# Feed-forward weights turned by transposing DMAs behind the output stores, with the first matrix in four column blocks, in place of TensorE transposes

## The chip, the core and the metric

One core of one Trainium2 chip. The metric is the device time of one execution in microseconds. A profiled execution has a span (first to last instruction) and a time of its own, which is a little longer. TensorE's clock has two levels, 1.2 and 2.4 GHz; the profile gives the granted clock of a stretch as a share of full speed.

## What is computed

A decoder layer with layer normalisation after each of three parts, for x of 16 x 256 x 512 in float32:

```python
x = _layernorm(x + attn(x, ...))               # gated long convolution (Hyena)
x = _layernorm(x + xattn(ctx, ctx, x, ...))     # state-space kernel, 32 heads of 8 rows
x = _layernorm(x + ffn(x, w1, w2))

def _bitlinear(x, w):                           # w1: 2048 x 512, w2: 512 x 2048
    rms = rsqrt(max(mean(w * w), EPS))
    w_quant = clip(round(w * rms), -1, 1) / rms
    scale = 127 / max(max(abs(x), -1), EPS)
    x_quant = clip(round(x * scale), -128, 127) / scale
    return einsum('bsd,fd->bsf', x_quant, w_quant)
# ffn: _bitlinear(gelu(_bitlinear(x, w1)), w2)
```

The weights are thus -1, 0 or 1 times a scalar. TensorE contracts over partitions, so both matrices must lie in SBUF transposed: w1 with its 512 input dims on partitions (4 groups of 128), w2 with its 2048 (16 groups).

## The kernel before

It runs as two blocks of five engine programs, one behind the other with a barrier of all engines between. `hyena_block` computes the first part, in two halves of 128 batch rows (HALF = 2), and leaves its result in HBM (`x1_scratch`). `heads_block` does the second and third part in a software pipeline over 32 heads. The change lies in the last stage of `hyena_block`, in the second half.

**A half.** 24 slots (two per group of 128 channels and kind x1, v, x0) project x with f16 matmuls (L509), ScalarE and VectorE form the short convolution, and for each of four channel groups a long convolution goes through HBM (`regroup`, `bring_back`). Then 16 output tokens follow. For each token R, TensorE multiplies y by `wout_t` into one of four half banks of `slot_bank` (`out_part`, L546; a float32 matmul is two records, so eight of a token); the first three of four partial products of tokens 0 to 3 are made ahead. `out_part(R)` waits until VectorE has added token R - 4. VectorE adds the residual row group `res` (L857), measures it (L859, L861), GpSimd makes the inverse deviation (L1050, L1052), and VectorE normalises one token later (L866). `res` has four buffers.

**SP's queue in this stage** (L446 to L454) is a hand-written order: for each t, `load_res(R + 3)`, which waits until the store of token R - 1 has landed, then `store_res(R)`, which waits for L866. All DMAs of the kernel are issued by SP and share one hardware queue. Ahead of the stage stand the loads of the weight parts 2 to 6 and of the first ctx, toeplitz and x1 data of the next block; part 7 is loaded at t = 0.

**The weights.** The two matrices go in eight parts of 128 x 2048 float32 (four of w1, four of w2). In the second half's slots ScalarE squares them for the mean; later each part is loaded again into `part_raw[i]` (buffers that are free by then), ScalarE rounds it (`round_part`, L749; the rounded number stands in the low half word of the float32), and VectorE clips it (`clip_part`, L954; parts 2 to 7 behind tokens 1 to 6). Then TensorE turns it: `turn_part(i)` (L589 to L601) does 16 transposes of 128x128 f16 into two PSUM banks behind token t = 1 + i (`PART_AT`), and ScalarE copies both halves out (`copy_part`, L751 to L760), subtracting the offset 1536, into `w1_t` or `w2_t`, which lie over `x_hi` and `x_lo`. ScalarE's order is round part i + 2, copy part i. Behind the last token `turn_first_ctx` and `convolve_first` do the first pieces of the next block in the same banks.

**The second block** turns its activations with transposing DMAs: `turn_xq` (L1328, 128x512 f16) and `turn_hq` (L1332, twice 128x1024 f16 a head), fed by ScalarE's `pack_xq` and `pack_hq` (L1538, L1515), which are passes of the same form as the new `pack_part`. `ffn1` (L1442) reads `w1_t` in rows of 512, `ffn2` (L1421) reads `w2_t`.

Of the kernel before, what the change touches and what calls it, by code (L numbers as in the profile page):

```python
# [6 lines left out]
ACT = mybir.ActivationFunctionType  # L7
AX_X = mybir.AxisListType.X
F32 = mybir.dt.float32
F16 = mybir.dt.float16  # L10
# [3 lines left out]
P = 128  # L14
T, B, D = 16, 256, 512
DC = D // P
E = 3 * D
EC = E // P
F = 2048
FC = F // P  # L20
# [4 lines left out]
HALF = B // P  # L25
# [13 lines left out]
HALF_ONE = 1536.0  # L39
# [3 lines left out]
def view(ap, offset, *dims):  # L43

    return bass.AP(ap.tensor, ap.offset + offset, [ap.ap[0], *[list(d) for d in dims]])
# [3 lines left out]
def hyena_block(nc, w, early, dram):  # L49
# [8 lines left out]
    NSLOT = 2 * 3 * DC  # L58
# [14 lines left out]
    PARTS = 4  # L73
    with ExitStack() as ctx:
# [6 lines left out]
        def sem(name):  # L81
            return ctx.enter_context(nc.semaphore(name))
# [6 lines left out]
        x_hi, x_lo = w["x_hi"], w["x_lo"]  # L89
# [3 lines left out]
        v_tok = sb("v_tok", [P, P * T])  # L93
# [33 lines left out]
                    *[view(w[name][:, :, :].bitcast(F32), 0, (1, F)) for name in ("w_hi", "w_lo")],  # L127
                    view(u[:, :, :], 0, (1, F)), view(conv_all[:, :, :, :], X0 * F, (1, F))]

        turn_bank = [view(early["conv_bank"][i // 2][:, i % 2, :], 0, (P, 4), (1, P)) for i in range(4)]  # L130
        slot_bank = [ps(f"slot_bank{i}", [P, 2, 512]) for i in range(2)]

# [13 lines left out]
        slot_full = sem("slot_full")  # L146
# [7 lines left out]
        c_stored = sem("c_stored")  # L154
        c_loaded = sem("c_loaded")
        ch_full = sem("ch_full")
        ch_copied = sem("ch_copied")
# [44 lines left out]
        inv_made = sem("inv_made")  # L202
        clipped = sem("clipped")
        rounded = sem("rounded")
        part_turned = sem("part_turned")
        part_done = sem("part_done")

        def quad_buf(Q):
# [6 lines left out]
        TOTAL_AT, SUM_MATRIX_AT, MEAN_AT, INVERSE_AT = 18, 19, 20, 21  # L215
        ROUND_AT = {21: 0, 23: 1}
        CLIP_AT = {i - 1: i for i in range(2, 2 * PARTS)}
        PART_AT = {1 + i: i for i in range(2 * PARTS)}
        CTX_AT, PAIRS_AT = 11, 12

        TURN_AT = {4: 1, 9: 2, 14: 3}
# [47 lines left out]
        with nc.Block() as block:  # L269
            @block.sync  # L270
            def _(sp):
# [66 lines left out]
                def load_part(i):  # L338
# [12 lines left out]
                        sp.wait_ge(y_done, 4 * HALF * DC)  # L351
                    sp.dma_start(part_target(i, part_raw[i]), part_source(i)).then_inc(part_loaded[i], 16)

                def load_w_in(cc):
                    for k in range(KINDS):
                        e = k * DC + cc
                        sp.dma_start(raw_w_in(KINDS * cc + k), dram["W_in"][e * P:(e + 1) * P, :]).then_inc(win_loaded[cc], 16)
# [53 lines left out]
                for hf in range(HALF):  # L411
# [34 lines left out]
                    for t in range(T):  # L446
                        R = hf * T + t
                        if R + 3 < HALF * T:
                            load_res(R + 3)
                        store_res(R)  # L450
                        if hf + 1 < HALF and t in LOAD_QUAD_AT:
                            load_quad(NQ * (hf + 1) + LOAD_QUAD_AT[t])
                        if hf + 1 == HALF and t == 0:
                            load_part(2 * PARTS - 1)  # L454

            @block.tensor
            def _(pe):
# [128 lines left out]
                    pe.wait_ge(ch_copied, 4 * (HALF * DC - 1))  # L586
                    nc.tensor.matmul(turn_bank[0][:, 0, 0:2], ones[:, :], total[:, :], start=True, stop=True).then_inc(summed, 1)

                def turn_part(i):  # L589
                    pe.wait_ge(clipped, i + 1)  # L590
                    low = view(part_raw[i].bitcast(F16), 0, (2, F))
                    for hh in range(2):
                        if i >= 2:
                            pe.wait_ge(part_done, 2 * (i - 2) + hh + 1)
                        elif hh == 0:
                            pe.wait_ge(ch_copied, 4 * HALF * DC)
                        out = turn_bank[2 * (i % 2) + hh][:, :, :].rearrange("p a b -> p (a b)").bitcast(F16)
                        for j in range(FC // 2):
                            fc = hh * FC // 2 + j
                            last = nc.tensor.transpose(out[:, j * P:(j + 1) * P], low[:, fc * P:(fc + 1) * P], w["ident16"][:, :])  # L600
                        last.then_inc(part_turned, 1)  # L601

                def turn_first_ctx():
                    pe.wait_ge(early["ctx_reversed"], 1)
                    pe.wait_ge(part_done, 2 * (2 * PARTS - 2) + 1)
                    for lb in range(LB):
                        last = nc.tensor.transpose(turn_bank[0][:, lb, :], early["ctx_rev"][:, 0, lb * P:(lb + 1) * P], w["ident"][:, :])
                    last.then_inc(early["ctx_turned"], 1)

                def convolve_first(tb):  # L610

                    if tb == 0:
                        pe.wait_ge(early["toep_loaded"][0], 16)
                        pe.wait_ge(early["kv_done"], 1)
                        pe.wait_ge(part_done, 2 * 2 * PARTS)
                    for sb_ in range(tb + 1):
                        for hh in range(2):
                            last = first_conv(nc, early, turn_bank[2 * tb + hh][:, :, :].rearrange("p a b -> p (a b)"), tb, sb_, hh)
                    last.then_inc(early["conv_full"], 1)
# [7 lines left out]
                for hf in range(HALF):  # L627
# [25 lines left out]
                        out_part(hf * T + t, range(DC - 1))  # L653
                    for t in range(T):
                        out_part(hf * T + t, range(DC) if t >= PARTIAL else [DC - 1])
                        if hf + 1 == HALF and t in PART_AT:
                            turn_part(PART_AT[t])
                        if hf + 1 == HALF and t == CTX_AT:
                            turn_first_ctx()
                        if hf + 1 < HALF and t in QUAD_AT:  # L660
                            turn_quad(NQ * (hf + 1) + QUAD_AT[t])
# [5 lines left out]
            def _(act):  # L667
# [80 lines left out]
                    m = i // PARTS  # L748
                    nc.scalar.activation(part_raw[i], part_raw[i], ACT.Copy, scale=rms[:, m:m + 1], bias=LOW_HALF).then_inc(rounded, 1)  # L749

                def copy_part(i):  # L751
                    for hh in range(2):
                        act.wait_ge(part_turned, 2 * i + hh + 1)
                        bank = turn_bank[2 * (i % 2) + hh][:, :, :].rearrange("p a b -> p (a b)").bitcast(F16)
                        if i < PARTS:
                            out = view(w["w1_t"], (4 * i + 2 * hh) * P, (P, 2), (F, DC), (1, P))
                        else:
                            out = view(w["w2_t"], hh * (FC // 2) * D + (i - PARTS) * P, (D, FC // 2), (1, P))
                        src = view(bank, 0, (DC * P, 2), (P, DC), (1, P)) if i < PARTS else view(bank, 0, (P, FC // 2), (1, P))
                        nc.scalar.activation(out, src, ACT.Copy, bias=-HALF_ONE).then_inc(part_done, 1)  # L760

                norm_first(0)
                split_hi(0)
# [28 lines left out]
                for i in range(2 * PARTS):  # L792
                    if i + 2 < 2 * PARTS:
                        round_part(i + 2)
                    copy_part(i)
                for h in range(2):
                    act.wait_ge(early["ctx_loaded"][h], 16)
                    reverse_blocks(nc, early, h).then_inc(early["ctx_reversed"], 1)
# [367 lines left out]
def heads_block(nc, w, early, dram):  # L1166
# [6 lines left out]
    with ExitStack() as ctx:  # L1173
# [115 lines left out]
        with nc.Block() as block:  # L1289
# [72 lines left out]
            def _(pe):  # L1362
# [61 lines left out]
                def ffn1(head, k):  # L1424
# [14 lines left out]
                    else:  # L1439
                        pe.wait_ge(g_done, head.count(4, 2))  # L1440
                    for dc in range(DC):
                        last = nc.tensor.matmul(bank[:, :], xq_t[:, dc, :], w["w1_t"][:, dc, k * 512:(k + 1) * 512],  # L1442
                                                start=(dc == 0), stop=(dc == DC - 1))
                    last.then_inc(ff1_full, 1)

# [352 lines left out]
def build(nc, dram):  # L1798
    with ExitStack() as ctx:
# [6 lines left out]
            "block_diag": sb("block_diag", [P, GROUPS, P]),  # L1806
            "x_hi": sb("x_hi", [P, DC, T * P], F16), "x_lo": sb("x_lo", [P, DC, T * P], F16),
        }
        w["w1_t"] = w["x_hi"][:, :, :]
        w["w2_t"] = w["x_lo"][:, :, :].rearrange("p c (k e) -> p (c k) e", e=D)  # L1810

        early = {name: view(w["block_diag"][:, :, :], n * 2 * L, *dims) for n, (name, dims) in enumerate((
# [59 lines left out]
```

## Time and profile before

| | us |
|---|---|
| median of 3 runs | 1064.82 (1059.51 to 1065.6) |
| the profiled execution | 1063.69 |
| its span | 1061.9 |
| TensorE matmul / weight load, busy | 1006.2 / 602.9 |
| VectorE / ScalarE / GpSimd, busy | 799.3 / 599.9 / 552.7 |

In the rows below, times are in us from the span's start and mean durations in ns unless marked. PE is TensorE's matmuls, PEld its weight loads, DVE VectorE, ACT ScalarE, POOL GpSimd, SPq SyncE's queue of DMA issues. A row of the timeline has start, duration, engine, line, operation, output<-input, count, and in square brackets the idle time before it with what ended it. The profile names, for a wait on several semaphores, the one that came last. A row of the windows has the stretch, its length, each engine's busy time with the count of instructions, then the granted clock, the mean busy share of the 16 DMA engines, and GB/s.

### The profile page before, as it was taken

What the parts mean: (1) busy time and instruction counts of PE and PEld (TensorE: products, weight loads), DVE (VectorE), ACT (ScalarE), POOL (GpSimd) and SP (SyncE); (2) the same over time, 40 slices, a digit from 0 to 9 for tenths busy, and PEclk for the clock granted to TensorE, in tenths of its full rate; (3) what the DMA queues carried; (4) which work ended last, traced back from release to release, by engine and by line L of the source; (5) the groups of instructions that cost most, each with busy time, mean ns of one, the idle gap of its engine ahead of it and who ended that gap; (6) DMA issues with size and microseconds to landing.
All of it is one profiled execution on the core that took longest, in us unless ns stands there. A gap on an engine that the chain in (4) does not pass through costs nothing.

```text
span 1061.9 us, 14827 instructions
## 1 busy us (share of the span) xinstructions
PE 1006.2 (95%) x4679; PEld 602.9 (57%) x4679; DVE 799.3 (75%) x1509; ACT 599.9 (56%) x728; POOL 552.7 (52%) x886
## 2 busy tenths in 40 slices
PE   3899999999999999978999999999999999999985
PEld 2455545544445555456666666666666666666641
DVE  7967975786475567657888888888888888888862
ACT  5655544112566558114666666767576767676664
POOL 5320310221000004269787887878787878787861
PEclk9999999999999999989999999999999999999998
DMA  9323655456475777441444544444444444444334
GB/s 322 61 60 120 203 152 163 145 165 194 162 227 189 241 259 255 141 143 51 105 98 113 105 113 108 115 106 117 104 117 105 109 114 101 122 99 114 76 64 91
DMA packets 178220, 144.65 MB, mean 136 GB/s; under 512 B 99988, under 2 KB 132792, under 8 KB 176120
## 3 DMA queue, kind: packets, MB, share of 16 engines
q1 hardware_dynamic: 178168, 144.00, 49.3%
q8 instruction: 27, 0.44, 0.2%
q14 instruction: 25, 0.20, 0.1%
HBM read 89.29 MB, written 33.70 MB: 116 GB/s over the span
## 4 chain that ended last, share of the span: by engine, by line
PE 50%; DVE 2%; POOL 1%; ACT 1%; DMA 1%; issue 1%; POOLq 0%; DVEq 0%; ACTq 0%
PE conv_bank L1398 28%; PE hq_bank L1421 9%; PE ff_bank L1442 5%; PE back_bank L1442 5%; PE back_bank L1412 1%; PE back_bank L1381 1%; PE ctx_bank L1369 1%; DMA hq_t<-hq_int 0%; POOL sum L1742 0%; DVE z L1607 0%; DVE g_max L1674 0%; POOL sum L1744 0%; ACT g L1546 0%; DMA xq_t<-xq_int 0%; ACT hq_f L1507 0%
## 5 line engine op out<-in xcount | busy, mean ns | idle before, releaser
L1742 POOL TENSOR_TENSOR sum<-z 128x640 f32<-128x640 f32 x128 | 198.2, 1549 | 11.6 <-DVE z L1619 9.6
L837 DVE SCALAR_TENSOR_TENSOR conv_all<-u,taps,conv_all 128x1024 f32<-128x1024 f32 x92 | 122.4, 1331 | 93.2 <-ACT conv_all L708 91.4
L1398 PE MATMUL conv_bank<-block_diag 128*128 128x288 f32 x628 | 167.8, 411 | 1.8 <-DVE z L1619 1.8
L1398 PE MATMUL conv_bank<-kv,block_diag 128*128 128x288 f32 x640 | 168.6, 406 | 0.9 <-DVE z L1619 0.8
L1398 PEld LDWEIGHTS conv_bank<-kv,block_diag 128*128 128x128 f32 x640 | 117.8, 190 | 31.6 <-DVE z L1619 1.8
L1398 PEld LDWEIGHTS conv_bank<-block_diag 128*128 128x128 f32 x628 | 117.3, 193 | 32.4 <-DVE z L1619 2.2
L1421 PE MATMUL hq_bank<-x_lo,hq_t 128*128 128x512 f16 x512 | 122.2, 382 | 4.7 <-DMA hq_t<-hq_int 4.7
L1674 DVE TENSOR_REDUCE g_max<-g 128x1 f32<-128x512 f32 x128 | 85.8, 673 | 41.5 <-ACT g L1546 41.5
L700 ACT ACTIVATE u<-slot_bank,bias,unscale 128x1024 f32<-128x1024 f32 x46 | 55.4, 1204 | 108.9 <-PE slot_bank L509 88.6
L1744 POOL TENSOR_TENSOR sum<-sum 128x320 f32<-128x320 f32 x128 | 111.3, 869 | 10.0
L1607 DVE TENSOR_TENSOR z<-conv_bank,qx 128x512 f32<-128x512 f32 x128 | 88.0, 687 | 34.2 <-PE conv_bank L1398 24.6
L546 PE MATMUL slot_bank<-wout_t,y 128*128 128x512 f32 x256 | 112.8, 594 | 0.0
L1520 ACT ACTIVATE x<-x,a_shift,a_rstd 128x512 f32<-128x512 f32 x32 | 26.0, 814 | 134.9 <-POOL a_shift L1763 134.9
L509 PE MATMUL slot_bank<-x_hi,w_hi 128*128 128x512 f16 x384 | 91.8, 381 | 3.8 <-ACT conv_all L708 2.1
L509 PE MATMUL slot_bank<-x_lo,w_hi 128*128 128x512 f16 x384 | 91.2, 379 | 3.5 <-DVE x_lo L825 3.5
L509 PE MATMUL slot_bank<-x_hi,w_lo 128*128 128x512 f16 x384 | 91.9, 382 | 0.0
L1050 POOL TENSOR_SCALAR r_rstd<-r_meanvar 128x1 f32<-128x1 f32 x32 | 19.7, 614 | 134.2 <-DVE r_meanvar L861 134.2
L1421 PEld LDWEIGHTS hq_bank<-x_lo,hq_t 128*128 128x128 f16 x512 | 50.1, 98 | 64.8 <-DMA hq_t<-hq_int 6.5
L546 PEld LDWEIGHTS slot_bank<-wout_t,y 128*128 128x128 f32 x256 | 47.6, 190 | 54.3 <-issue 54.0
L1507 ACT ACTIVATE hq_f<-g,h_scale 128x1024 f32<-128x1024 f32 x64 | 73.0, 1141 | 2.0 <-DVE h_scale L1669 2.0
L1442 PE MATMUL ff_bank<-x_hi,xq_t 128*128 128x512 f16 x256 | 66.6, 383 | 3.4 <-DMA xq_t<-xq_int 3.4
L1616 DVE TENSOR_TENSOR z<-conv_bank,qx 128x384 f32<-128x384 f32 x128 | 69.3, 542 | 0.0
(181 smaller groups left out, 1676.2 us busy)
## 6 DMA issues: line engine op xcount, KB each, us to landing
x_quad<-in_w SPq DMA_DIRECT2D x10, 1024.0 KB, 8.3
v_scratch<-conv_all SPq DMA_DIRECT2D x16, 512.0 KB, 3.5
c_scratch<-v_tok SPq DMA_DIRECT2D x8, 1024.0 KB, 5.3
y<-c_scratch SPq DMA_DIRECT2D x8, 1024.0 KB, 4.9
res<-in_x SPq DMA_DIRECT2D x32, 256.0 KB, 2.9
x_scratch<-res SPq DMA_DIRECT2D x32, 256.0 KB, 3.1
block_diag<-in_ctx SPq DMA_DIRECT2D x32, 256.0 KB, 3.7
block_diag<-ssm_scratch SPq DMA_DIRECT2D x32, 256.0 KB, 3.7
```

The lines of the kernel that those rows point to most:

```text
L509: last = nc.tensor.matmul(slot_bank[n % 2][:, q, :], wt[:, dc, e * P:(e + 1) * P], xt[:, dc, cols], start=(j == 0 and dc == 0), stop=(j == ...
L546: last = nc.tensor.matmul(slot_bank[R // 2 % 2][:, R % 2, :], y[:, cc, t, :], w["wout_t"][:, cc, :], start=(cc == 0), stop=(cc == DC - 1))
L837: ins = nc.vector.scalar_tensor_tensor(out=acc, in0=(u_first[kind] if n < 3 else u)[:, t0 + tap:t0 + tap + T // 2, :].rearrange("p t b -> ...
L1398: last = nc.tensor.matmul(view(conv_bank[tb % 2][:, hh, :], 0, (ROW64, T // 2), (1, PAIRS)), toep[:, head.buf, (tb - sb_) * P:(tb - sb_ + ...
L1421: last = nc.tensor.matmul(hq_bank[:, :], hq_t[:, fc, :], w["w2_t"][:, fc, :], start=(fc == 0), stop=(fc == FC - 1))
L1442: last = nc.tensor.matmul(bank[:, :], xq_t[:, dc, :], w["w1_t"][:, dc, k * 512:(k + 1) * 512], start=(dc == 0), stop=(dc == DC - 1))
L1507: nc.scalar.activation(hq_f[:, half], g[:, half], ACT.Copy, scale=h_scale[:, 0:1], bias=LOW_HALF).then_inc(hq_rounded, 1)
L1607: nc.vector.tensor_tensor(view(z[:, b, :, :], 0, (4 * PLANE, T), (PLANE + 1, 4), (1, HD)), view(conv, 0, (ROW64, T), (HD, 4), (1, HD)), vi ...
L1616: nc.vector.tensor_tensor(view(z[:, b, :, :], DN, (4 * PLANE, T), (PLANE, 3), (1, HD)), view(conv, HD, (ROW64, T), (HD, 3), (1, HD)), view ...
L1674: nc.vector.tensor_reduce(g_max[:, k:k + 1], g[:, k * 512:(k + 1) * 512], AX_X, ALU.max, apply_absolute_value=True).then_inc(g_maxed, 1)
L1742: nc.gpsimd.tensor_tensor(sum2[:, :, :], z[:, b, :, 0:half], z[:, b, :, half:2 * half], ALU.add).then_inc(sum2_done, 1)
L1744: nc.gpsimd.tensor_tensor(sum1[:, :, :], sum2[:, :, 0:PLANE], sum2[:, :, PLANE:half], ALU.add).then_inc(sum1_done, 1)
```

## The change

Each part, once clipped, is packed by ScalarE (`pack_part`) into f16 in SBUF, into a buffer that is free by then (`part_int`: v_tok, and then the first half of the raw buffer of the part before). SP then issues one transposing DMA per part (`turn_part`, now in SP's program) from there into `w1_t` or `w2_t`, at the end of the iterations t = 2 to 9. `w1_t` is laid out as [k, dc, 512] in place of [dc, k x 512], and for w1 the pack puts the four 128-column blocks of a row group in the order in which the DMA can write them in one run. TensorE's 128 transposes and ScalarE's 16 copies from PSUM are removed, with the waits of `turn_first_ctx` and `convolve_first` on them. SP waits at the end of its program for all eight.

```diff
@@ -126,6 +126,8 @@
                     *[view(conv_all[:, :, :, :], n * F, (1, F)) for n in (X1, V)],
                     *[view(w[name][:, :, :].bitcast(F32), 0, (1, F)) for name in ("w_hi", "w_lo")],
                     view(u[:, :, :], 0, (1, F)), view(conv_all[:, :, :, :], X0 * F, (1, F))]
+
+        part_int = [view(home, 0, (1, F // 2)).bitcast(F16) for home in (v_tok[:, :], *part_raw[:-1])]
 
         turn_bank = [view(early["conv_bank"][i // 2][:, i % 2, :], 0, (P, 4), (1, P)) for i in range(4)]
         slot_bank = [ps(f"slot_bank{i}", [P, 2, 512]) for i in range(2)]
@@ -202,7 +204,7 @@
         inv_made = sem("inv_made")
         clipped = sem("clipped")
         rounded = sem("rounded")
-        part_turned = sem("part_turned")
+        packed = sem("packed")
         part_done = sem("part_done")
 
         def quad_buf(Q):
@@ -215,7 +217,7 @@
         TOTAL_AT, SUM_MATRIX_AT, MEAN_AT, INVERSE_AT = 18, 19, 20, 21
         ROUND_AT = {21: 0, 23: 1}
         CLIP_AT = {i - 1: i for i in range(2, 2 * PARTS)}
-        PART_AT = {1 + i: i for i in range(2 * PARTS)}
+        TURN_PART_AT = {2 + i: i for i in range(2 * PARTS)}
         CTX_AT, PAIRS_AT = 11, 12
 
         TURN_AT = {4: 1, 9: 2, 14: 3}
@@ -350,6 +352,17 @@
                     elif i == 7:
                         sp.wait_ge(y_done, 4 * HALF * DC)
                     sp.dma_start(part_target(i, part_raw[i]), part_source(i)).then_inc(part_loaded[i], 16)
+
+                def turn_part(i):
+
+                    if i == 0:
+                        sp.wait_ge(slot_full, HALF * NSLOT)
+                    sp.wait_ge(packed, i + 1)
+                    if i < PARTS:
+                        out = view(w["w1_t"], i * DC * 512, (P, FC), (1, P))
+                    else:
+                        out = view(w["w2_t"], (i - PARTS) * P, (D, FC), (1, P))
+                    sp.dma_start_transpose(out, part_int[i]).then_inc(part_done, 16)
 
                 def load_w_in(cc):
                     for k in range(KINDS):
@@ -452,6 +465,9 @@
                             load_quad(NQ * (hf + 1) + LOAD_QUAD_AT[t])
                         if hf + 1 == HALF and t == 0:
                             load_part(2 * PARTS - 1)
+                        if hf + 1 == HALF and t in TURN_PART_AT:
+                            turn_part(TURN_PART_AT[t])
+                sp.wait_ge(part_done, 2 * PARTS * 16)
 
             @block.tensor
             def _(pe):
@@ -586,23 +602,9 @@
                     pe.wait_ge(ch_copied, 4 * (HALF * DC - 1))
                     nc.tensor.matmul(turn_bank[0][:, 0, 0:2], ones[:, :], total[:, :], start=True, stop=True).then_inc(summed, 1)
 
-                def turn_part(i):
-                    pe.wait_ge(clipped, i + 1)
-                    low = view(part_raw[i].bitcast(F16), 0, (2, F))
-                    for hh in range(2):
-                        if i >= 2:
-                            pe.wait_ge(part_done, 2 * (i - 2) + hh + 1)
-                        elif hh == 0:
-                            pe.wait_ge(ch_copied, 4 * HALF * DC)
-                        out = turn_bank[2 * (i % 2) + hh][:, :, :].rearrange("p a b -> p (a b)").bitcast(F16)
-                        for j in range(FC // 2):
-                            fc = hh * FC // 2 + j
-                            last = nc.tensor.transpose(out[:, j * P:(j + 1) * P], low[:, fc * P:(fc + 1) * P], w["ident16"][:, :])
-                        last.then_inc(part_turned, 1)
-
                 def turn_first_ctx():
                     pe.wait_ge(early["ctx_reversed"], 1)
-                    pe.wait_ge(part_done, 2 * (2 * PARTS - 2) + 1)
+                    pe.wait_ge(ch_copied, 4 * HALF * DC)
                     for lb in range(LB):
                         last = nc.tensor.transpose(turn_bank[0][:, lb, :], early["ctx_rev"][:, 0, lb * P:(lb + 1) * P], w["ident"][:, :])
                     last.then_inc(early["ctx_turned"], 1)
@@ -612,7 +614,6 @@
                     if tb == 0:
                         pe.wait_ge(early["toep_loaded"][0], 16)
                         pe.wait_ge(early["kv_done"], 1)
-                        pe.wait_ge(part_done, 2 * 2 * PARTS)
                     for sb_ in range(tb + 1):
                         for hh in range(2):
                             last = first_conv(nc, early, turn_bank[2 * tb + hh][:, :, :].rearrange("p a b -> p (a b)"), tb, sb_, hh)
@@ -653,8 +654,6 @@
                         out_part(hf * T + t, range(DC - 1))
                     for t in range(T):
                         out_part(hf * T + t, range(DC) if t >= PARTIAL else [DC - 1])
-                        if hf + 1 == HALF and t in PART_AT:
-                            turn_part(PART_AT[t])
                         if hf + 1 == HALF and t == CTX_AT:
                             turn_first_ctx()
                         if hf + 1 < HALF and t in QUAD_AT:
@@ -748,16 +747,19 @@
                     m = i // PARTS
                     nc.scalar.activation(part_raw[i], part_raw[i], ACT.Copy, scale=rms[:, m:m + 1], bias=LOW_HALF).then_inc(rounded, 1)
 
-                def copy_part(i):
-                    for hh in range(2):
-                        act.wait_ge(part_turned, 2 * i + hh + 1)
-                        bank = turn_bank[2 * (i % 2) + hh][:, :, :].rearrange("p a b -> p (a b)").bitcast(F16)
-                        if i < PARTS:
-                            out = view(w["w1_t"], (4 * i + 2 * hh) * P, (P, 2), (F, DC), (1, P))
-                        else:
-                            out = view(w["w2_t"], hh * (FC // 2) * D + (i - PARTS) * P, (D, FC // 2), (1, P))
-                        src = view(bank, 0, (DC * P, 2), (P, DC), (1, P)) if i < PARTS else view(bank, 0, (P, FC // 2), (1, P))
-                        nc.scalar.activation(out, src, ACT.Copy, bias=-HALF_ONE).then_inc(part_done, 1)
+                def pack_part(i):
+
+                    act.wait_ge(clipped, i + 1)
+                    if i == 0:
+                        act.wait_ge(c_stored, 16 * HALF * DC)
+                    else:
+                        act.wait_ge(packed, i)
+                    low = view(part_raw[i].bitcast(F16), 0, (2, F))
+                    if i < PARTS:
+                        out, src = view(part_int[i], 0, (DC * P, DC), (P, DC), (1, P)), view(low, 0, (2 * P, DC), (2 * D, DC), (2, P))
+                    else:
+                        out, src = part_int[i], low
+                    nc.scalar.activation(out, src, ACT.Copy, bias=-HALF_ONE).then_inc(packed, 1)
 
                 norm_first(0)
                 split_hi(0)
@@ -792,7 +794,7 @@
                 for i in range(2 * PARTS):
                     if i + 2 < 2 * PARTS:
                         round_part(i + 2)
-                    copy_part(i)
+                    pack_part(i)
                 for h in range(2):
                     act.wait_ge(early["ctx_loaded"][h], 16)
                     reverse_blocks(nc, early, h).then_inc(early["ctx_reversed"], 1)
@@ -1439,7 +1441,7 @@
                     else:
                         pe.wait_ge(g_done, head.count(4, 2))
                     for dc in range(DC):
-                        last = nc.tensor.matmul(bank[:, :], xq_t[:, dc, :], w["w1_t"][:, dc, k * 512:(k + 1) * 512],
+                        last = nc.tensor.matmul(bank[:, :], xq_t[:, dc, :], w["w1_t"][:, k, dc, :],
                                                 start=(dc == 0), stop=(dc == DC - 1))
                     last.then_inc(ff1_full, 1)
 
@@ -1806,7 +1808,7 @@
             "block_diag": sb("block_diag", [P, GROUPS, P]),
             "x_hi": sb("x_hi", [P, DC, T * P], F16), "x_lo": sb("x_lo", [P, DC, T * P], F16),
         }
-        w["w1_t"] = w["x_hi"][:, :, :]
+        w["w1_t"] = view(w["x_hi"][:, :, :], 0, (DC * 512, F // 512), (512, DC), (1, 512))
         w["w2_t"] = w["x_lo"][:, :, :].rearrange("p c (k e) -> p (c k) e", e=D)
 
         early = {name: view(w["block_diag"][:, :, :], n * 2 * L, *dims) for n, (name, dims) in enumerate((
```

## Rows read from the trace of the kernel before

**Rows 1.** The page: busy time by engine, and the chain that ended last.
```profile
PE 1006.2 (95%) x4679; PEld 602.9 (57%) x4679; DVE 799.3 (75%) x1509; ACT 599.9 (56%) x728; POOL 552.7 (52%) x886
...
PE 50%; DVE 2%; POOL 1%; ACT 1%; DMA 1%; issue 1%; POOLq 0%; DVEq 0%; ACTq 0%
```

**Rows 2.** Waits from 411 to 462 us, then VectorE's timeline.
```profile
DVE res L857 <- DMA res<-in_x: 15.5, 13, 2.9
...
429.26 0.69 DVE L857 TENSOR_TENSOR res<-slot_bank,res 128x512 f32<-128x512 f32 x1 [1.35 <-DMA res<-in_x]
...
455.76 0.69 DVE L857 TENSOR_TENSOR res<-slot_bank,res 128x512 f32<-128x512 f32 x1 [1.35 <-DMA res<-in_x]
```

**Rows 3.** Timeline of SP's queue of DMA issues.
```profile
411.84 0.33 SPq L283 DMA_DIRECT2D res<-in_x  x1
...
429.87 0.33 SPq L283 DMA_DIRECT2D res<-in_x  x1
430.24 0.43 SPq L288 DMA_DIRECT2D x_scratch<-res  x1
433.37 0.33 SPq L283 DMA_DIRECT2D res<-in_x  x1
...
440.75 0.43 SPq L288 DMA_DIRECT2D x_scratch<-res  x1
445.79 0.33 SPq L283 DMA_DIRECT2D res<-in_x  x1
```

**Rows 4.** Line L288, the stores: time from issue to landing.
```profile
DMA to landing us min/median/max: 2.0/3.1/7.6
```

**Rows 5.** Timeline of TensorE: token 8, the turn of part 7, token 9.
```profile
424.21 3.65 PE L546 MATMUL slot_bank<-wout_t,y 128*128 128x512 f32 x8
427.70 1.06 PE L600 MATMUL conv_bank<-ident,conv_all 128*128 128x128 f16 x16
428.59 3.65 PE L546 MATMUL slot_bank<-wout_t,y 128*128 128x512 f32 x8
```

**Rows 6.** Timeline of ScalarE, then lines L1515 and L1538 (min/median/max ns).
```profile
393.47 1.99 ACT L749 ACTIVATE conv_all<-conv_all,rms 128x2048 f32<-128x2048 f32 x1
...
423.96 1.94 ACT L760 ACTIVATE x_lo<-conv_bank 128x1024 f16<-128x1024 f16 x2 [1.60 <-PE conv_bank L600]
...
L1515 ACT ACTIVATE hq_int<-hq_f x64: 1045/1057/1060, 505.4 to 1047.0; 128x1024 f16<-128x1024 f16 x64
...
L1538 ACT ACTIVATE xq_int<-xq_f x32: 629/630/631, 486.0 to 1033.0; 128x512 f16<-128x512 f16 x32
```

**Rows 7.** The transposing DMAs of 1024 and 512 columns, and one's stretch.
```profile
L1332 SPq DMA_TRANSPOSE hq_t<-hq_int x64: 1232/1252/2031, 506.5 to 1048.1; - x64
...
DMA to landing us min/median/max: 3.0/3.1/4.8
...
L1328 SPq DMA_TRANSPOSE xq_t<-xq_int x32: 1190/1213/1324, 486.6 to 1033.7; - x32
...
DMA to landing us min/median/max: 2.4/2.4/2.5
...
503.20:504.40 1.20, 1.20 (x8) 1.00 (x8) 1.10 (x6) 0.19 (x1) 1.06 (x2) 1.00 0.48 107
```

**Rows 8.** Windows: eight tokens of the output stage.
```profile
412.00:440.00 28.00, 27.73 (x124) 14.15 (x123) 20.01 (x36) 15.68 (x16) 12.27 (x16) 1.00 0.53 159
```

**Rows 9.** Timeline of SP's queue in the first half, around a 1 MB load.
```profile
204.54 0.43 SPq L276 DMA_DIRECT2D x_quad<-in_x  x1
207.58 0.33 SPq L283 DMA_DIRECT2D res<-in_x  x1
...
213.90 0.33 SPq L283 DMA_DIRECT2D res<-in_x  x1
```

**Rows 10.** Windows: TensorE's granted clock around the start of the second block.
```profile
456.20:459.90 3.70, 0.00 (x0) 0.00 (x0) 2.11 (x5) 0.00 (x0) 1.00 (x3) 0.86 0.26 97
...
466.00:468.00 2.00, 2.00 (x5) 1.43 (x5) 0.00 (x0) 0.00 (x0) 1.84 (x4) 0.50 0.72 215
```

## The prediction

> **What bounds the kernel now.** I read the page first: TensorE is busy for 1006.2 us of 1061.9, and the chain of waits gives it half of the span [rows 1]. That makes "less work on TensorE" look like time won. But the share is an average, and the change acts in one stage only, the last 16 output tokens of the first block (from 399 to 459 us), where the eight parts of the weights are turned. So I read that stage by its waits, then in order of time.
>
> In this stage VectorE's addition of the residual (L857), one per token, waits in 13 of 16 tokens, and each time for the same thing: the DMA that brings the residual row group into `res`. From token 8 (429.26) to token 15 (455.76) it never finds the row there early [rows 2]. TensorE is ahead of it: its last output matmul of token 8 ends near 427.7, 1.5 us before VectorE takes it up, and that with all eight turns in its stream.
>
> What sets the pace of these loads is SP's own order, `load_res(R + 3)`, `store_res(R)`: a load needs the buffer that the store of token R - 1 empties. The load at 429.87 is followed by the store at 430.24, and the next load goes out at 433.37, which is 3.1 us behind that store, the median time to landing of such a store [rows 3, 4]. So a token costs 0.37 + 3.1 = 3.5 us, whatever TensorE does. TensorE spends 427.70 - 424.21 = 3.5 us on a token and its wait for the bank, and 0.89 on a turn [rows 5]. Two places in the row depart from 3.5: up to 411.84 the DMA engines work off the weights and early context loads (I give this stretch no change: none of its transfers is touched), and the store at 440.75 takes 5.0 us, so that the next load comes at 445.79 [rows 3]. That straggler is worth 5.4 - 3.5 = 1.9 us here.
>
> **The change part by part.**
>
> *TensorE loses the turns.* A turn of one part takes 0.89 us of its stream (427.70 to 428.59) [rows 5]; eight make 7.1 us. Because from token 3 on VectorE takes tokens at the pace of the loads, and the four banks let TensorE run at most four tokens ahead, TensorE stands idle for those 7.1 us instead. Value at the end of the block: 0; were TensorE the pacer it would be -7.1.
>
> *ScalarE packs in place of copying.* Two copies of about 1 us from PSUM go (the pair at 423.96 takes 1.94), one pass of 128x2048 comes. The nearest rows are `pack_hq`, 1.06 us for 1024 columns, and `pack_xq`, 0.63 for 512, so 0.43 per 512 more and 1.06 + 2 x 0.43 = 1.9 us for 2048 [rows 6]. Even. ScalarE's waits for TensorE in this stage (1.60 before that pair) go too; it waits for the clips instead, which stay where they are in VectorE's order. Part 7 is clipped before VectorE takes up token 8 at 429.26 [rows 2], so the last pack is done by 431.2 at the latest. Nothing waits for ScalarE there. Value 0.
>
> *SP gets eight transposing DMAs*, one at the end of each of the iterations t = 2 to 9, behind `store_res(t)`. Their waits first: they would be reached from about 416.5 (t = 2) to 441 (t = 9), and the packs are done from 397 (part 0, behind the rounding that ends at 395.5 [rows 6], + 1.9) to 431 (part 7), some 10 us earlier or more. So SP doesn't stop at `packed`. If it did, the loads and stores of all later tokens would stand behind it, microsecond for microsecond. Issuing: 1.21 us for 512 columns, 1.25 for 1024 [rows 7]; for 2048 I take 1.3 (by the same step; the other end is 4 x 1.21 = 4.9, if the issue went by size). It falls into the 3.1 us in which SP waits for the store anyway. Value 0 by the first; by the second the turn's issue ends 0.43 (the store's own issue) + 4.9 = 5.3 us behind the store, 2.2 more than 3.1, and eight add +18. I hold that far off, since doubling the size adds 0.04.
>
> *The data that they move* is the term that counts. A turn of 512 columns (128 KB) keeps the 16 DMA engines 0.48 x 1.20 = 0.58 us at full share and moves 107 GB/s x 1.2 us, which is all of it [rows 7]. A part has 2048 columns, so 4 x 0.58 = 2.3 us; by the landing times (3.1 for 1024 columns, 2.4 for 512) each 512 more take 0.7, so 2.8. I take 2.45. The loads and stores of eight tokens take 0.53 x 28 us, 1.85 a token [rows 8]. Together 4.3 us of work a token, more than the 3.5 in which a token goes by now. In order of time: the store goes out at 0, the turn's data runs behind it from about 2 to 4.5, the next load and store (issued at 3.1 and 3.5) come behind it and land near 7.4, in place of 6.6. So a token costs 4.3 for as long as a turn stands in each, and the eight add 8 x 0.8 = +6.4 us. Low end: 0, if the turn's data slips into the pauses of the engines (they are idle for half of the time [rows 8]). High end by the nearest row of a big transfer at the same place: the 1 MB load of `x_quad` issued at 204.54 behind a store in the first half; the period after it is 213.90 - 207.58 = 6.3, which is 2.8 more than 3.5 [rows 9]. Half its size at its rate: 1.4 each, +11; at its full price +22.
>
> The Trainium skill would have this term vanish. "Advanced Engine Details and Errata", section "X-Bar Transpose (TRN2)", says that such DMAs are about as fast as plain ones and expects 350 to 400 GB/s; a part would then take about 1.4 us as an estimate by that page, 3.3 with the token's own traffic, less than 3.5, and the time would stay. The trace speaks against it: over the whole stretch with any traffic of the 128 KB turn the engines are counted at 0.58 us, some 225 GB/s [rows 7].
>
> *TensorE's clock.* In the 3.7 us in which TensorE stands idle before the second block the granted clock is 0.86 on average, and it is at 0.50 (the 1.2 GHz level) still in 466 to 468 [rows 10]. After the change TensorE finishes the first block earlier against VectorE, so it idles longer before the same start; the start is at the low level already. Value 0; were the low level to last 4 us longer, up to 2 us more.
>
> *The new order of the first matrix* (column blocks) leaves each matmul's 512 columns contiguous; the second block reads, waits and issues as before. Value 0. The last transfer of a turn is issued about six tokens before the block's end, so the new last wait of SP is over when it is reached.
>
> **Sum.** 1063.69 (the profiled execution: span 1061.9 and 1.8 around it) + 6.4 = 1070.1 us. The median of the three runs is 1064.82, so this is 0.5% slower. A measurement of this kernel tells about 1% from no change.
>
> **The rivals.**
>
> A. *The turns pace the loads* (the forecast): a turn of 2.3 to 2.8 us of data adds 0.65 to 1.15 a token, so 1069 to 1073, or from 1067 on if the straggler is absent; 1070.1 at the price taken.
>
> B. *Hidden in the pauses.* The engines' share is only 0.53 here [rows 8], and the store is issued ahead of the turn. If the turn's data is through before the next store's turn comes, the token stays at 3.5: 1063.7, or 1061.8 if the straggler at 440.75 is absent. It takes a turn of under 3.5 - 1.85 = 1.65 us, against 2.3 by the row. By the page of the Trainium skill named above this would be the outcome.
>
> C. *The turns cost as the big load did*, 1.4 or more each, since reads and writes of three transfers in a queue mix badly: 1063.7 + 11 = 1075, at the full 2.8 each 1086. The second matrix's turns write 16 separate pieces of 128 elements into each partition, which no row shows.
>
> D. *TensorE is the pacer after all* and its 7.1 us come off: 1056.6; this is the side of faster. For it: tokens 4 to 8 took TensorE 4.4 us each with the turn. Against it: VectorE's waits name the load in all of them [rows 2]. It decides only if the loads land before the matmuls; they would have to be 0.9 us quicker per token.
>
> E. *The change doesn't get its cover*: a turn is not ready or its issue grows with the size, and SP stands still in front of loads and stores: +18, 1082.
>
> **How the numbers follow.** A 0.52, B 0.24, C 0.13, D 0.06, E 0.05. Slower by over 1% is above 1075.5: E with 0.05, two thirds of C (whose first price lies just under it) with 0.09, a little of A with 0.01, so 0.15. Faster by over 1% is below 1054.2, more than D gives: 0.03. Within 1%: 0.82. The range takes in B and, above, C's first price: 1060 to 1078.
>
> **What would show it.** Right: SP's issue rows hold eight transposing DMAs at 1.3 us each from t = 2; the loads at their side follow each other at 4.2 to 4.4 us and return to 3.5 from t = 10; DMA share above 0.9 in this stretch; VectorE still waits for `res<-in_x`; TensorE shows pauses for `slot_bank`; ScalarE's pack takes 1.9; the second block starts near 466 in place of 459.9 and lasts as long as before. Wrong: a cadence of 3.5 beside the turns (B) or 4.9 and more (C), stores landing later than 3.1 in iterations without a turn, or a second block that changes in length, which no step here foresees.

## The result, and the profile after

| | before | changed |
|---|---|---|
| median of six runs, us | 1065.38 (1059.51 to 1066.35) | 1072.11 (1070.84 to 1073.59) |
| ratio | | 1.0071, 95% interval 1.0047 to 1.0094 |
| profiled execution / its span | 1063.69 / 1061.9 | 1073.59 / 1071.8 |

The changed kernel is 0.7% slower. TensorE's counted busy time falls by 1.4 us, not by the 7.1 us of its turns, and the span is 9.9 us longer. The 1.4 says little by itself: over the profiles below that have the same 4551 matmul records, the busy time varies from 998.3 to 1005.1 us. First the page of the changed kernel (busy time, DMA queue), for [rows 1]:

```profile
PE 1004.8 (94%) x4551; PEld 598.6 (56%) x4551; DVE 799.9 (75%) x1509; ACT 600.5 (56%) x720; POOL 552.9 (52%) x886
...
q1 hardware_dynamic: 194808, 148.19, 51.0%
```

The 4.19 MB more than before in the queue (144.00 MB there) are the eight turns, 512 KB each. The timeline of SP's queue shows what they do to the loads, for [rows 3]:

```profile
413.86 0.33 SPq L285 DMA_DIRECT2D res<-in_x  x1
...
417.84 0.33 SPq L285 DMA_DIRECT2D res<-in_x  x1
418.21 0.43 SPq L290 DMA_DIRECT2D x_scratch<-res  x1
418.75 3.60 SPq L365 DMA_TRANSPOSE x_hi<-v_tok  x1
422.41 0.56 SPq L285 DMA_DIRECT2D res<-in_x  x1
...
452.48 2.95 SPq L365 DMA_TRANSPOSE x_lo<-u  x1
455.48 0.94 SPq L285 DMA_DIRECT2D res<-in_x  x1
...
459.81 0.33 SPq L285 DMA_DIRECT2D res<-in_x  x1
460.18 0.43 SPq L290 DMA_DIRECT2D x_scratch<-res  x1
463.26 0.33 SPq L285 DMA_DIRECT2D res<-in_x  x1
```

From 417.84 to 455.48 there are eight periods, each with a turn: 4.7 us each in place of 3.5. Behind the last turn one period of 4.3 follows, then 3.45 (459.81 to 463.26). What was not foreseen is the turn's own issue, 2.8 to 4.0 us instead of 1.3: in six of the eight periods store, turn and load stand in SP's queue without a pause, and the load goes out as soon as the issue of the turn has ended. The windows of that stretch, and the waits from 411 to 470 us, for [rows 8] and [rows 2]:

```profile
417.84:455.48 37.64, 30.19 (x70) 12.16 (x68) 19.60 (x37) 10.28 (x8) 11.22 (x16) 1.00 0.95 214
```
```profile
DVE res L859 <- DMA res<-in_x: 24.2, 12, 3.3
...
PE slot_bank L562 <- DVE res L859: 6.4, 6, 1.3
```

The DMA engines went from a share of 0.53 to 0.95. VectorE still waits for the residual loads, and longer. TensorE, 7.1 us of work lighter, now waits 6.4 us for VectorE to free a bank. ScalarE's pack takes 1.9 us, as worked out, and waits for nothing that matters (ScalarE's timeline, for [rows 6]):

```profile
429.18 1.91 ACT L762 ACTIVATE u<-conv_all 128x2048 f16<-128x2048 f16 x1 [3.21 <-DVE conv_all L956]
```

Where the 9.9 us of span came from: 2.0 stood already at the first undisturbed load (413.86 against 411.84), before any turn; 8.5 came in the stage (from that load to the second block's first transposes, 56.6 us against 48.1); and the second block is 0.6 shorter (601.4 against 602.0). The 2.0 are spread between executions: in the profiles of the ten experiments the same load lies anywhere from 408.67 to 414.79. So the stage is the better measure of one profile, and the medians (6.7 apart) are the fair total; the changed kernel's profile is the slowest of its six runs. The eight periods alone make 8 x 1.2 = 9.6. The straggler of 1.9 us in [rows 3] is absent here, and absent in e1 and e4 too, where SP's order of loads and stores is the same.

### The profile page after: what moved, and what is told of

Read it like the earlier page. It is cut to its first block, busy times and chain, and to the rows that moved or that the text cites. A ratio compares the mean times of both kernels' runs of the same rounds, so it can differ in the third digit from the quotient of the medians.

```text
span 1071.8 us, 14573 instructions
## 1 busy us (share of the span) xinstructions
PE 1004.8 (94%) x4551; PEld 598.6 (56%) x4551; DVE 799.9 (75%) x1509; ACT 600.5 (56%) x720; POOL 552.9 (52%) x886
## 4 chain that ended last, share of the span: by engine, by line
PE 50%; DVE 2%; POOL 1%; ACT 1%; DMA 1%; issue 0%; POOLq 0%; DVEq 0%; ACTq 0%
PE conv_bank L1400 27%; PE hq_bank L1423 10%; PE ff_bank L1444 5%; PE back_bank L1444 5%; PE back_bank L1414 1%; PE back_bank L1383 1%; PE ctx_bank L1371 1%; POOL sum L1744 0%; DVE z L1609 0%; DMA hq_t<-hq_int 0%; DVE g_max L1676 0%; POOL sum L1746 0%; ACT g L1548 0%; DMA xq_t<-xq_int 0%; POOL z L1778 0%
```

## The experiments

"Cadence" is the mean distance of the residual loads over eight periods beside the turns (where there are none, over the same tokens). "The block starts" is the second block's first transpose on TensorE: at 459.93 in the profile before, at 470.42 in the changed kernel's. All diffs are against the changed kernel unless said.

**e1_no_turns.** The eight transposing DMAs and their last wait are left out, so the feed-forward weights are never put in place; all the rest runs as in the changed kernel.

```diff
-                        if hf + 1 == HALF and t in TURN_PART_AT:
-                            turn_part(TURN_PART_AT[t])
-                sp.wait_ge(part_done, 2 * PARTS * 16)
```

> The eight transposing DMAs and the wait for them are left out (so the feed-forward weights are never put in place); TensorE's transposes are gone as in the changed kernel and ScalarE still packs. If the turns pace the loads (engines' work or SP's issue), the loads of res go out every 3.5 us through the whole stage again, and the time is that of the kernel before within its noise, 1062 to 1066: taking 7.1 us of work from TensorE is worth nothing. The rival, that TensorE's transposes were the pacer and the turns hide that gain, expects 1057 or less.

Measured: 1062.97 us, ratio to before 1.0005 (0.9986 to 1.0025). Its queue (timeline of SP):

```profile
429.12 0.33 SPq L285 DMA_DIRECT2D res<-in_x  x1
429.49 0.43 SPq L290 DMA_DIRECT2D x_scratch<-res  x1
432.56 0.33 SPq L285 DMA_DIRECT2D res<-in_x  x1
```

The cadence is 3.5 again. So the loss lies in the DMAs, and taking the transposes from TensorE is worth nothing in this kernel (within the interval). Rival D is out.

**e2_two_halves.** The same data at the same places, each turn cut into two DMAs.

```diff
-                    sp.dma_start_transpose(out, part_int[i]).then_inc(part_done, 16)
+                    for h in range(2):
+                        half = slice(h * FC // 2, (h + 1) * FC // 2)
+                        sp.dma_start_transpose(out[:, half, :], part_int[i][:, h * F // 2:(h + 1) * F // 2]).then_inc(part_done, 16)
```

> Each turn is issued as two DMAs of 1024 columns at the same place, the same data in all. Theory of the engines' work: the data sets the pace, so the cadence of the loads stays at 4.5 to 4.8 us beside the turns and the time at 1070 to 1074, however the issue is cut. Rival, issue by size: a DMA of 2048 columns costs SP 3.6 us because of its form, one of 1024 costs 1.25; two make 2.5, which fits into the 3.1 us of the store, and the cadence falls to 3.5 to 3.8, the time to 1064 to 1067.

Measured: 1069.57 us, 1.0052 (1.0035 to 1.0069). Timeline of SP and the windows of the stretch:

```profile
416.33 0.33 SPq L285 DMA_DIRECT2D res<-in_x  x1
416.70 0.43 SPq L290 DMA_DIRECT2D x_scratch<-res  x1
417.24 2.99 SPq L367 DMA_TRANSPOSE x_hi<-v_tok  x2
420.27 1.07 SPq L285 DMA_DIRECT2D res<-in_x  x1
...
450.93 0.78 SPq L285 DMA_DIRECT2D res<-in_x  x1
```
```profile
416.33:450.93 34.60, 30.34 (x70) 12.17 (x69) 19.50 (x36) 10.46 (x8) 11.21 (x16) 1.00 1.02 232
```

The cadence is 34.6 / 8 = 4.3 us, which is the sum of the prediction (2.45 + 1.85), with the engines' share at 1.02. That is a little under what was expected of the engines' work (4.5 to 4.8, 1070 to 1074). Issue by size would have given 3.5 to 3.8 and is out. In the two profiles one DMA of 2048 columns costs 0.4 a token more than two of 1024 with the same data, but the times don't confirm it: 1.0052 and 1.0071 have intervals that overlap.

**e3_act_issues.** SP's queue keeps loads and stores only; ScalarE issues the turns.

```diff
+                    if i >= 4:
+                        act.wait_ge(res_added, T + i + 1)
+                        turn_part(i - 4)
...
+                for i in range(4, 2 * PARTS):
+                    act.wait_ge(res_added, T + i + 5)
+                    turn_part(i)
```

> The same eight turns at about the same times, but issued from ScalarE's queue, so that SP's queue holds only loads and stores. Engines' work: SP is free, the engines still have about 4.5 us of work for a token, and the loads go out every 4.3 to 4.7 us; 1070 to 1074. Rival, SP's issue: SP no longer stands still, cadence 3.5, 1064 to 1066. If a second queue lets loads and stores pass the turns, the cadence lies near 3.5 as well, but then a turn lands later than 5.5 us.

Measured: 1076.34 us, 1.0122 (1.0105 to 1.0139). Timelines of SP and of ScalarE's queue:

```profile
425.22 0.33 SPq L285 DMA_DIRECT2D res<-in_x  x1
425.60 0.45 SPq L290 DMA_DIRECT2D x_scratch<-res  x1
430.34 0.33 SPq L285 DMA_DIRECT2D res<-in_x  x1
```
```profile
424.71 1.72 ACTq L760 DMA_TRANSPOSE x_hi<-x_quad  x1
```

SP is free, the turn's issue is short (1.4 to 2.2 us), and the cadence is 5.1, worse than in the changed kernel. A store issued at 425.60 lands only 4.7 us later. So the loss stays when SP is freed of the long issue. The expectation (4.3 to 4.7, 1070 to 1074) missed as well: that the second queue would be dearer by 0.4 a token than the first was in neither theory. Nor were the engines at their fullest: their share over the eight periods is 0.90, with 206 GB/s (windows):

```profile
414.98:455.83 40.85, 30.39 (x71) 12.43 (x69) 21.18 (x41) 10.57 (x8) 11.78 (x18) 1.00 0.90 206
```

**e4_turns_last.** The turns alone, behind the last store.

```diff
-                        if hf + 1 == HALF and t in TURN_PART_AT:
-                            turn_part(TURN_PART_AT[t])
+                for i in range(2 * PARTS):
+                    turn_part(i)
                 sp.wait_ge(part_done, 2 * PARTS * 16)
```

> All eight turns stand at the end of SP's program, behind the last store, with nothing beside them. Engines' work: the first is issued in about 1.3 us, since the queue is empty, and the later ones are held back to the pace of their data, some 2.5 us each; the second block starts 20 to 23 us after the last store, total near 1085. Issue by size: every one, the first too, is issued in 3 to 4 us, total near 1095. The loads of the stage go out every 3.5 us either way.

Measured: 1081.34 us in its one run (expected near 1085). Timeline of SP, and the windows of nearly all of it:

```profile
455.18 2.21 SPq L365 DMA_TRANSPOSE x_hi<-v_tok  x1
457.45 5.05 SPq L365 DMA_TRANSPOSE x_hi<-x_quad  x2
462.54 2.40 SPq L365 DMA_TRANSPOSE x_hi<-conv_all  x1
...
472.30 2.46 SPq L365 DMA_TRANSPOSE x_lo<-u  x1
```
```profile
455.18:474.70 19.52, 0.00 (x0) 0.00 (x0) 0.00 (x0) 0.00 (x0) 0.00 (x0) 0.50 1.09 209
```

Eight turns take from 455.18 to 474.76, 2.45 us each: the price taken in the prediction. Every turn lands 4.7 to 5.0 us after its issue began and the engines' share is 1.09, so they are held to the pace of their data. The first was expected at 1.3 us and took 2.2. But its queue was not empty: the last store had been issued at 454.76, 0.4 us before. In ScalarE's queue, which held nothing else in this stage (e3), the same turns were issued in as little as 1.35 us. So no run shows that the issue itself grows much from 1024 columns (1.25) to 2048. The loads of the stage kept 3.6. The second block starts at 477.61, some 23 us after the last store was issued, as expected (20 to 23).

**e5_spread.** Half turns as in e2, one a token, with four of them where no load follows. The schedule of the edit:

```diff
-        TURN_PART_AT = {2 + i: i for i in range(2 * PARTS)}
+        TURN_HALVES_AT = {**{t: (t - 1,) for t in range(1, 13)}, 13: (12, 13), 14: (14, 15)}
```

> The turns as sixteen DMAs of 1024 columns, one behind each store from t = 1 to 12 and two each at t = 13 and 14, where no load follows. Engines' work: half a turn is 1.2 us, with the token's own 1.85 it makes 3.1, less than the 3.5 of a token, so it is hidden: cadence of the loads 3.5 to 3.6, time 1062 to 1066, the changed kernel's loss gone with all its data still moved. Rival, that a transposing DMA in the queue costs each token a fixed delay whatever its size: 12 tokens at some 0.5 to 0.8 each, 1069 or more.

Measured: 1069.82 us, 1.004 (1.0022 to 1.0058). The expectation was wrong, and the time is the one that the rival gave (1069 or more), though not by its fixed delay of 0.5 to 0.8 a token. The cadence is (449.91 - 408.67) / 11 = 3.75, not 3.5, so 2.7 us; and the end of the stage is a new wait (timelines of SP, and of TensorE):

```profile
452.90 3.35 SPq L366 DMA_TRANSPOSE x_lo<-w_lo  x2
456.29 0.58 SPq L290 DMA_DIRECT2D x_scratch<-res  x1
456.92 2.74 SPq L366 DMA_TRANSPOSE x_lo<-u  x2
459.70 0.63 SPq L290 DMA_DIRECT2D x_scratch<-res  x1
```
```profile
462.27 1.09 PE L1385 MATMUL back_bank<-ident,block_diag 128*128 128x128 f32 x4 [9.87 <-PEq L271]
```

VectorE's last normalisation ended at 456.3, but the last stores stand in SP's queue behind four half turns: the block starts 6.0 us later instead of 0.8. "No load follows" was not enough; the stores and the barrier follow.

**e6_spread_swap, e7_before_swap, e8_after_swap, e9_no_turns_swap.** Four kernels with one more edit, the order of SP's queue in the second half: the store of token R goes out before the load of R + 3, so it no longer waits until the store before it has landed. e6 is e5 with it, e7 the kernel before, e8 the changed kernel, e9 is e1 (again without any turn, the weights not put in place).

```diff
                     for t in range(T):
                         R = hf * T + t
+                        if hf + 1 == HALF and t >= 1:
+                            store_res(R)
                         if R + 3 < HALF * T:
                             load_res(R + 3)
-                        store_res(R)
+                        if hf + 1 < HALF or t == 0:
+                            store_res(R)
```

> As e5_spread, and in the second half the store of token R stands ahead of the load of R + 3 in SP's queue, so that a store no longer waits for the landing of the one before. If SP's chain of store and load is the pacer of the stage, the cadence falls from 3.5 to 3.1 to 3.3 (then bound by the engines' 3.1 and the path normalise, store, load, add over three tokens) and the time to 1058 to 1062, since TensorE, without the transposes, can follow. Rival, that something else sets 3.5 (TensorE's 3.43 for a token, VectorE): no gain against e5_spread.

> The kernel before with the same exchange of store and load and nothing else. The loads' cadence falls as in e6_spread_swap, but now TensorE with its transposes ends token 15 only at 453 and becomes the pacer at the end: VectorE adds token 15 some 2 us earlier than before, 1061 to 1063. If it is as fast as e6_spread_swap, taking the transposes from TensorE is worth nothing even then; if not, the difference is what it is worth, at most 4 us.

> The changed kernel with the exchange. Engines' work: the engines are full beside the turns (share 0.95), so the order in the queue can give little: cadence 4.3 to 4.6 over the eight tokens, then shorter; time 1067 to 1071. Rival, SP's order and issue set 4.7: cadence falls to 4.0 or less, time 1065 or less.

> As e1_no_turns (the eight transposing DMAs and the wait for them left out, so the feed-forward weights are never put in place), with the store ahead of the load as in e7_before_swap. It shows what taking the transposes from TensorE is worth once the loads no longer pace the stage. In e7_before_swap VectorE waited 8.8 us for TensorE; without the transposes that goes, and the time should be 1 to 4 us under e7_before_swap (1056 to 1059). Rival: the loads and stores pace it at 3.1 us anyway and it is no faster than e7_before_swap, 1060.

Measured:

| | us | ratio to before, interval | cadence | block starts |
|---|---|---|---|---|
| e6_spread_swap | 1061.60 | 0.9979 (0.9963 to 0.9994) | 3.1 | 456.65 |
| e7_before_swap | 1059.99 | 0.9954 (0.9936 to 0.9972) | 3.3 | 454.91 |
| e8_after_swap | 1065.00 | 1.0003 (0.9988 to 1.0018) | 4.1 | 459.44 |
| e9_no_turns_swap | 1055.28 | 0.9922 (0.9900 to 0.9943) | 2.9 | 451.09 |

SP's chain was the pacer of the stage before: exchanging two lines of its queue gives 0.46%, somewhat more than expected (1059.99 against 1061 to 1063). In e7 VectorE's wait is now for TensorE (waits from 405 to 472 us of e7, for [rows 2]):

```profile
DVE res L860 <- PE slot_bank L549: 8.8, 7, 2.3
...
DVE res L860 <- DMA res<-in_x: 4.4, 3, 2.7
```

So once the loads are out of the way, TensorE's transposes do cost: e9 is 0.32% (3.4 us) faster than e7. The difference is only just clear of noise (0.04 to 0.60% by the two intervals, an estimate). And the turns cost more than that: e8, with them whole, is 0.8% above e9. In e8 the queue (timeline of SP, windows) is full at 4.1 a token:

```profile
421.69 0.42 SPq L285 DMA_DIRECT2D res<-in_x  x1
422.16 2.97 SPq L365 DMA_TRANSPOSE x_hi<-x_quad  x1
425.17 0.58 SPq L290 DMA_DIRECT2D x_scratch<-res  x1
425.80 0.43 SPq L285 DMA_DIRECT2D res<-in_x  x1
```
```profile
413.67:446.65 32.98, 30.70 (x73) 12.62 (x71) 20.45 (x37) 11.11 (x8) 11.41 (x17) 1.00 1.02 246
```

e8 was expected at 1067 to 1071 with a cadence of 4.3 to 4.6. It came out at 4.1 and at 1065.00, which is the time that the rival gave (SP's order and issue set 4.7: 4.0 or less, 1065 or less). Besides, with the exchange the loads behind the last turn catch up (446.65, 448.42, 452.44: 2.9 apart on average), so part of the delay is made good before the stage ends.

Put side by side, the cadences without TensorE's transposes part the two causes. A whole turn in each token costs 1.2 us with either order: 3.5 to 4.7 (e1, changed kernel) and 2.9 to 4.1 (e9, e8). The order costs 0.6 with or without turns. So the 4.7 was not the least that this data takes: the changed kernel moved 214 GB/s, e8 the same turns at 246, e6 its half turns at 265. Theory and rival of e8 each had a part of it.

**e10_even_swap.** As e6, with two half turns at t = 3, 6, 9 and 12 and one at the others up to 11.

```diff
-        TURN_HALVES_AT = {**{t: (t - 1,) for t in range(1, 13)}, 13: (12, 13), 14: (14, 15)}
+        TURN_HALVES_AT = {t: (j, j + 1) if t % 3 == 0 else (j,) for t in range(1, 13) for j in [t - 1 + (t - 1) // 3]}
```

> As e6_spread_swap, but all sixteen half turns lie in the iterations t = 1 to 12 (two at every third), so that none stands at the end of the stage. In e5_spread and e6_spread_swap the second block began 5 to 6 us after VectorE's last normalisation, in place of 1.3, because of the last four half turns; that tail should go. Four tokens then cost some 0.6 to 1.0 us more. Net 1058 to 1061, as fast as e7_before_swap or a little faster. If the engines' work is what counts and not the place, no gain against e6_spread_swap (1061.6).

Measured: 1058.16 us, 0.9959 (0.9942 to 0.9976). Cadence 3.3; the block starts at 453.49, and VectorE's last normalisation is at

```profile
452.08 0.55 DVE L873 TENSOR_SCALAR res<-res,r_meanvar,r_rstd 128x512 f32<-128x512 f32 x1 [0.77 <-POOL r_rstd L1059]
```

so the tail is gone (0.9 us from its end to the block; 6.0 in e5, 4.5 in e6), and the time is within the expected 1058 to 1061. e10 and e7 both beat both kernels, and can't be told apart by their intervals. e7 is the smaller edit.

## Why the prediction was right, step by step

- *What bounds the stage* (SP's order of store and load, not TensorE): shown twice. Taking TensorE's 7.1 us away changes nothing that shows (e1); letting the store go first gives 0.46% with the transposes in place (e7).
- *TensorE loses the turns, value 0*: right (e1, 1.0005). It is 0 only while the loads pace the stage; behind e7's edit the same 7.1 us are worth 3.4 (e9 against e7).
- *ScalarE's packs, the waits on `packed`, the new matrix layout, the clock: value 0*: right. e1 has the packs and isn't slower than before. The second block takes 601.4 us after and 602.0 before; it takes 601.9 in e4, where TensorE stood idle for 27.3 us before it.
- *The turn's data, 2.45 us*: right in time, 2.45 alone (e4). It was the middle of two estimates, 2.3 by the engines' share and 2.8 by the landings, so the exact hit is luck. In e4 the share is above 1, so 2.45 us there are some 2.7 by the count by which the row of 512 columns gave 2.3.
- *The token beside a turn, 4.3 us*: the step that was mis-sized. It is 4.7 as the kernel has it, 4.3 when the turn goes out as two DMAs (e2), and 4.1 with the store ahead of the load (e8). The sum took the engines' work as the whole period; but without turns the period is 3.5 by SP's order at a share of only 0.53, and a turn adds 1.2 to it and not 0.8. So eight tokens cost 9.6 and not 6.4. That is just above rival A's span (0.65 to 1.15 a token) and just below C's first price (1.4), so the sign "loads at 4.2 to 4.4" failed. With it the profiled execution adds up: 1063.69 + 9.6 - 1.9 (the straggler, which the sum had kept) + 2.0 (there before the stage) = 1073.4, against 1073.59. The median, 1072.11, lies 2.0 above the forecast. That this is so close is partly luck: the sum started from a profile that had the straggler, which hides 1.9 of the missing 3.2.
- *Issuing, 1.3 us*: wrong for this queue. 2.2 right behind a store (e4), 2.8 to 4.0 beside the loads and stores; only in a queue of its own did it come down to 1.35 (e3). It did not become rival E's +18. That it is mostly waiting for the same engines is likely, not shown: freeing SP of it (e3) made the cadence longer.
- Rival B (hidden) is out by the cadence, and with it the rate of the Trainium skill's "Advanced Engine Details and Errata", section "X-Bar Transpose (TRN2)": 512 KB in 2.45 us with nothing but other turns beside it (e4) are 214 GB/s, not 350 to 400. Rival C's strided second matrix isn't dearer: its four turns were issued in 2.8 to 3.9 us, those of the first in 3.5 to 4.0.

Left open: why a turn of 2.45 us adds 1.2 to a token with either order; whether one DMA of 2048 columns really costs 0.4 us a token more than two of 1024 (engine share 0.95 against 1.02, 214 GB/s against 232, one profile each), and why; and why the second queue costs 0.4 more again. No run took these apart.

## What to carry to other kernels

Before moving work from the busiest engine to the DMA engines, ask who ends the wait in that stage: here it was a chain of store and load in a queue, and the transposes left an engine whose work cost nothing there for engines whose spare time per token (3.5 - 1.85 = 1.65 us) was less than a turn takes (2.45). Add up the DMA engines' work per step of the loop, the new transfer's at its own measured rate, and compare it with the step; place what is added in small pieces where the sum still fits, and not at the end, where stores and the barrier stand behind it. The cheapest gain lay in the queue's order: a store issued before the load that waits for its predecessor.

## What the runs showed of the hardware

- A transposing DMA's issue time on SP isn't a constant: 1.25 us for 1024 columns in the second block (median), 1.24 to 1.6 in this stage (e2, e5, e6); for 2048 columns 2.2 right behind a store and 2.2 to 2.7 behind another turn (e4), up to 4.0 beside loads and stores. From ScalarE's queue, with the loads and stores in SP's, 2048 columns took 1.35 to 2.24 (e3).
- The same transfers split over two issuing engines went slower (5.1 us a token, e3) than through one (4.7).
- The same eight turns with the same loads and stores moved at 214 GB/s or at 246 (changed kernel, e8), by the order of store and load in the queue alone.
- The clock at the start of the second block made no difference that shows: its first four transposes took 0.63 to 0.66 us in e7, e8 and e9 (granted clock 1.00, 0.86 and 1.00 in that stretch) and 1.08 or 1.09 in all the other profiles (0.50, the 1.2 GHz level), and the block lasted 604.3, 602.3 and 601.2 us in those three, 601.3 to 602.3 in the others.
